# Expert results scattered to token order by GpSimd in the expert stage, and loaded by plain DMA later

## What is computed

```
x = layernorm(x + attn0(x))      # 16 heads of 64, a mask j < i + 64, behind a small MLP
x = layernorm(x + experts(x))    # 16 experts, each token goes to its best 4
x = layernorm(x + attn1(x))      # 16 heads of 8, low-rank additions to the weights
x = layernorm(x + recurrent(x))  # gated state, one step for each sequence

def experts(x):
    logits = -dist2(x, keys) + x @ rw.T + rb
    topv, topi = top_k(logits, 4);  w = softmax(topv)
    y_e = gelu(x @ w1[e].T + b1[e]) @ w2[e].T + b2[e]
    return sum_k w[k] * y_{topi[k]}
```

## Time and profile before

| | |
|---|---|
| median of 3 runs | 1423.19 us (1420.87 to 1427.43) |
| profiled execution, span from first to last instruction | 1445.1 us |
| its mean granted TensorE clock | 0.960 |
| busy: PE, DVE, ACT, POOL | 1272.4, 1014.5, 931.4, 770.7 us |
| DMA | 110.98 MB in 149016 packets |

### The profile page before, as it was taken

The page is one execution under the profiler, slowest core; times in us unless marked ns, Lnnn a source line. Parts: engine busy times, 40 slices in busy tenths (PEclk is TensorE's granted clock), DMA queues, the critical chain, the costliest instruction groups (busy, mean ns, idle before and its releaser), DMA issues.

```text
span 1445.1 us, 36685 instructions
## 1 busy us (share of the span) xinstructions
PE 1272.4 (88%) x9756; PEld 971.6 (67%) x9756; DVE 1014.5 (70%) x3763; ACT 931.4 (64%) x2825; POOL 770.7 (53%) x981
## 2 busy tenths in 40 slices
PE   7999999999999999984899998996787788788973
PEld 3777776777777777764899998993455455455652
DVE  2677777777777777775677776766787677678835
ACT  5878777777777778772465665653565555556644
POOL 1557777777777777775222121235466666664132
PEclk9999999999999999997899999997899989999997
DMA  9612222221112222221222223222323223222102
GB/s 340 206 60 74 73 73 73 73 73 54 47 51 72 69 71 71 73 74 58 62 71 82 77 82 90 81 79 65 80 58 78 67 53 85 58 61 64 36 1 59
DMA packets 149016, 110.98 MB, mean 77 GB/s; under 512 B 12833, under 2 KB 137249, under 8 KB 148770
## 3 DMA queue, kind: packets, MB, share of 16 engines
q1 hardware_dynamic: 139842, 92.45, 22.0%
q0 software_dynamic: 8192, 16.79, 4.1%
q10 hardware_dynamic: 864, 0.39, 0.1%
HBM read 47.27 MB, written 61.93 MB: 76 GB/s over the span
## 4 chain that ended last, share of the span: by engine, by line
PE 60%; DVE 10%; issue 8%; ACT 7%; another core or an unknown queue 4%; DMA 3%; SPq 3%; DVEq 3%; ACTq 1%; POOL 0%; POOLq 0%
PE psum L911 9%; PE psum L922 8%; PE psum L798 6%; PE psum L835 6%; PE psum L853 5%; PE psum L746 4%; PE psum L815 3%; PE psum L753 3%; PE psum L947 3%; PE psum L747 3%; ACT wall L1183 2%; PE psum L935 2%; PE psum L1018 2%; ACT P L1153 2%
## 5 line engine op out<-in xcount | busy, mean ns | idle before, releaser
L554 POOL TENSOR_SCALAR P<-P,rinv 128x192 f32<-128x192 f32 (+1 forms) x384 | 308.5, 816 | 158.7 <-DVE rinv L1335 151.7
L1153 ACT ACTIVATE P<-shifted,least 128x192 f32<-128x192 f32 (+1 forms) x512 | 240.2, 470 | 100.6 <-DVE least L1321 99.1
L1175 ACT ACTIVATE hid<-psum,wA 128x128 f32<-128x128 f32 x576 | 164.4, 368 | 123.8 <-PE psum L911 120.2
L1512 DVE TENSOR_REDUCE mx<-psum 128x2 f32<-128x512 f32 x256 | 165.2, 687 | 66.4 <-PE psum L1018 42.3
L1321 DVE CUSTOM_DVE_ANT_0 shifted<-psum,band 128x192 f32<-128x192 f32 (+1 forms) x512 | 168.9, 385 | 27.5 <-PE psum L798 27.2
L598 POOL DMA_INDIRECT yk<-xs,posc x128 | 125.6, 981 | 107.4 <-DVE wA L1473 57.6
L1183 ACT ACTIVATE wall<-psum 128x1024 f32<-128x1024 f32 x128 | 130.8, 1022 | 65.7 <-PE psum L935 47.5
L911 PE MATMUL psum<-xgT,wA 128*128 128x128 f32 x1152 | 156.0, 279 | 2.0 <-ACT hid L1175 1.4
L922 PE MATMUL psum<-wB,hid 128*128 128x128 f32 x1152 | 152.6, 276 | 0.0
L911 PEld LDWEIGHTS psum<-xgT,wA 128*128 128x128 f32 x1152 | 143.3, 195 | 3.2 <-ACT hid L1175 1.8
L835 PEld LDWEIGHTS psum<-ident,P 128*128 128x128 f32 x1024 | 117.6, 141 | 35.8 <-issue 29.4
(11 more groups left out here) (261 smaller groups left out, 2537.0 us busy)
## 6 DMA issues: line engine op xcount, KB each, us to landing
xs<-zrow SPq DMA_DIRECT2D x34, 1024.0 KB
xg<-xs SPq DMA_DIRECT2D x144, 64.0 KB, 1.8
xs<-yrow SPq DMA_DIRECT2D x144, 64.0 KB
wall<-in_wall SPq DMA_DIRECT2D x1, 8232.0 KB, 36.3
qkd<-parts SPq DMA_DIRECT2D x64, 96.0 KB
kst<-qkd SPq DMA_DIRECT2D x22, 128.0 KB
qst<-qkd SPq DMA_DIRECT2D x22, 128.0 KB
wall<-qkd SPq DMA_DIRECT2D x20, 128.0 KB
```

Of the source, the lines that this page charges most:

```text
L554: g.tensor_scalar(x, x, rinv[:, par, n:n + 1], None, ALU.mult).then_inc(s["pn_ready"], 1)
L1153: last = sc.activation(P[:, par, it, h, 0:w], shifted[:, par, it, h, 0:w], ACT.Exp, scale=-1.0, bias=least[:, par, n:n + 1], accum_out=row ...
L1175: sc.activation(hid[:, n % 4, f, :], up(n, f), ACT.Gelu, bias=wA[:, n % 4, F + f:F + f + 1]).then_inc(s["hid_ready"], 1)
L1512: v.tensor_reduce(out=mx[:, :, h], in_=SB[(par + 1 + h) % 3].rearrange("q (i n) -> q i n", i=TT), axis=mybir.AxisListType.X, op=ALU.max).t ...
```

## The change

Each row of `xs` gets a 129th word, the slot of its result: token times four plus k, behind 2048 spare slots. POOL writes these numbers once at the start (`slots`), copies two of them per partition into the rows before each pair of scatters, and waits for the earlier scatters before that copy and for the copy behind it. Unused rows are filled from `empty`, which is zero and has spare slot numbers. In the experts POOL scatters `yrow` by the slots that came with `xg` into a new DRAM tensor `yd` in token order, one indirect DMA a tile; SP no longer stores. `xg` has ten buffers, since the slots are read late. The gathers go: SP loads a batch of 256 tokens with its four results each from `yd` in one plain transfer (`fetch`), four batches in the expert stage and twelve at the start of steps of the second attention. POOL's other work of the expert stage is put between the scatters, tile by tile, and SP's first stack loads are dealt out in seven places. SP reads a tile's row number just before its load. DVE no longer copies `pos` to `pos_all`. The diff, cut to its core:

```diff
+RC = D + 1
+PITCH = RC
+SPILL = 2 * E * GT
+XG = 10
...
+        slots = sb("slots", [128, B, TT, TOPK], i32, c=a)
-        x1c = sb("x1c", [128, TT, D], c=a)
+        x1c = sb("x1c", [128, TT, RC], c=a)
+        empty = sb("empty", [128, E, RC], c=a)
-        xg = sb("xg", [128, 4, D], c=e2)
+        xg = sb("xg", [128, XG, RC], c=e2)
...
-        xs = nc.dram_tensor("xs", (ROWS, D), fp32, kind="Internal").ap()
+        xs = nc.dram_tensor("xs", (ROWS, PITCH), fp32, kind="Internal").ap()
+        yd = nc.dram_tensor("yd", (SPILL + TOK * TOPK, D), fp32, kind="Internal").ap()
...
-                sp.dma_start(rows[128 * c:128 * c + 128, :, :], nothing).then_inc(s["filled"], 16)
-            sp.dma_start(xs[DUMMY:ROWS, :].rearrange("(e r) d -> r e d", r=128), nothing[:, 0:NT - FULL, :]).then_inc(s["filled"], 16)
+                sp.dma_start(rows[128 * c:128 * c + 128, :, :], empty[:, :, :]).then_inc(s["filled"], 16)
+            spare_rows = xs[DUMMY:ROWS, :].rearrange("(e r) d -> r e d", r=128)
+            sp.dma_start(spare_rows[:, :, 0:D], zrow[:, :].rearrange("q (o d) -> q o d", o=1).to_broadcast([128, NT - FULL, D])).then_inc(s["filled"], 16)
+            sp.dma_start(spare_rows[:, :, D:RC], spare_slot[:, 0:NT - FULL].rearrange("q (e o) -> q e o", o=1).bitcast(fp32), allow_slow_non_contiguous=True).then_inc(s["filled"], 16)
...
             def load_rows(n):
                 need_alone(sp, "tin_mm", n - 3)
-                row[n] = row_of(n)
-                sp.dma_start(xg[:, n % 4, :], xs[bass.ds(row[n], GT), :]).then_inc(s[f"xg_in{n % 4}"], 16)
-
-            def store_rows(n):
-
-                need_alone(sp, "yrow_ready", n + 1)
-                need_alone(sp, f"ys_out{n % 2}", 16 * (n // 2))
-                sp.dma_start(xs[bass.ds(row[n], GT), :], yrow[:, n % 4, :]).then_inc(s[f"ys_out{n % 2}"], 16)
+                if n >= XG:
+                    need_alone(sp, f"ys_out{n % 2}", 16 * ((n - XG) // 2 + 1))
+                row = row_of(n)
+                sp.dma_start(xg[:, n % XG, :], xs[bass.ds(row, GT), 0:RC]).then_inc(s[f"xg_in{n % 4}"], 16)
+
+            def fetch(b, par):
+
+                need_alone(sp, "comb_done", b + 2)
+                sp.dma_start(yk[:, (par + 1) % 3, :, :], yd[bass.ds(SPILL + (b + 4) * N * TOPK, N * TOPK), :].rearrange("(q n) d -> q n d", n=TT * TOPK)).then_inc(s["yk_in"], 16)
+
+            def stored(n):
+
+                for k in range(2):
+                    sp.wait_ge(s[f"ys_out{k}"], 8 * n)
...
-                if n in (98, 100, 102):
+                if 98 <= n < 98 + 14 and n % 2 == 0:
                     load_stack(-2, 0, (n - 98) // 2)
+                for b, at in ((-4, 40), (-3, 72), (-2, 104), (-1, 136)):
+                    if n == at:
+                        stored(at - 8)
+                        fetch(b, b % 3)
+            stored(NT)
 
             def attention(b, par):
+                if has(b, 4) and not (isinstance(b, int) and b < 0):
+                    fetch(b, par)
...
-                        for k in (2 * p, 2 * p + 1):
+                        need_alone(pool, "scat", 16 * TT * (TOPK * (b - 2) + p))
+                        g.tensor_copy(rows_of(b - 2)[:, :, D:RC].bitcast(i32), slots[:, bass.ds(b - 2, 1), :, p:p + 1].rearrange("q o i k -> q (o i) k")).then_inc(s["slot_ready"], 1)
+                        need_alone(pool, "slot_ready", TOPK * (b - 2) + (p + 1))
+                        for it in range(TT):
+                            n = TOPK * it + p
                             nc.gpsimd.indirect_dma_start(
-                                out=xs, out_offset=bass.IndirectOffsetOnAxis(pos[:, k:k + 1], 0),
-                                in_=rows_of(b - 2)[:, k // TOPK, :], in_offset=None).then_inc(s["scat"], 16)
+                                out=xs, out_offset=bass.IndirectOffsetOnAxis(pos[:, n:n + 1], 0),
+                                in_=rows_of(b - 2)[:, it, :], in_offset=None).then_inc(s["scat"], 16)
...
             def outputs(b, par):
                 deviations(b)
-                fetch(b, par, 0)
+                gates_of(b, par)
                 keep(b)
                 combine(b, par)
                 new_state(b)
-                fetch(b, par, 1)
...
+            def scatter(n):
+
+                need_alone(pool, "yrow_ready", n + 1)
+                need_alone(pool, f"ys_out{n % 2}", 16 * (n // 2))
+                g.indirect_dma_start(out=yd, out_offset=bass.IndirectOffsetOnAxis(xg[:, n % XG, D:RC].bitcast(u32), 0),
+                                     in_=yrow[:, n % 4, :], in_offset=None).then_inc(s[f"ys_out{n % 2}"], 16)
...
+            for n in range(NT):
+                scatter(n)
+                clear_ahead(n)
+                for b, first in ((-5, 37), (-4, 69), (-3, 101), (-2, 133)):
+                    if n == first:
+                        gates_of(b, b % 3)
...
-                        v.tensor_copy(pos_all[:, bass.ds((b - 1) * TT * TOPK, TT * TOPK)], posf[:, :])
```

More of the change, by code:

```diff
@@ L568, in ones_rows, with gates_of @@
                 g.memset(kst[k][MROW:MROW + NPART, h:h + count, :], 1.0)
[L570 to L605 removed]
+            def gates_of(b, par):
+                if has(b, 5):
+                    need_alone(pool, "comb_done", b + 3)
+                    g.tensor_copy(gcur[:, (par + 2) % 3, :], gate_all[:, bass.ds(b + 5, 1), :].rearrange("q o k -> q (o k)")).then_inc(s["gates_in"], 1)
             def deviations(b):
@@ new lines, in combine_ahead, with clear_ahead @@
+                if piece == TT:
+                    g.tensor_tensor(acc, y4[:, :, 0, :], y4[:, :, 1, :], ALU.add)
+                if piece == TT + 1:
+                    g.tensor_tensor(acc, acc, x_all[:, (b + 4) * TT:(b + 5) * TT, :], ALU.add).then_inc(s["comb_done"], 1)
+            def clear_ahead(piece):
+                if piece < 16:
+                    x, h = (qst, kst)[piece // 4 % 2][piece // 8], 4 * (piece % 4)
+                    g.memset(x[:, h:h + 4, :].rearrange("q h n -> q (h n)").bitcast(fp32), 0.0)
+                elif piece < 24:
+                    if piece == 16:
+                        g.drain()
+                    ones_rows((piece - 16) // 4, 4 * (piece % 4), 4)
+                elif piece < 30:
+                    if piece == 24:
+                        g.drain()
+                    g.memset(v32[:, (piece - 24) // TT, piece % TT, :, :], 0.0)
+                elif piece == 30:
+                    g.drain()
+                    g.memset(v32[:, :, :, :, DH1:DH1 + 1], 1.0).then_inc(s["cleared"], 1)
@@ new lines, in scatter @@
+            def scatter(n):
[3 more added lines that the diff above has]
+                                     in_=yrow[:, n % 4, :], in_offset=None).then_inc(s[f"ys_out{n % 2}"], 16)
+            pool.sem_inc(s["x3_kept"], 1)
+            for n in range(NT):
+                scatter(n)
[3 more added lines that the diff above has]
+                        gates_of(b, b % 3)
+                for b, first in ((-4, 63), (-3, 95), (-2, 127)):
+                    if first <= n < first + TT + 2:
+                        combine_ahead(b, n - first)
+                for b, first in ((-3, 73), (-2, 107)):
+                    if n == first:
+                        deviations(b)
+                    if n == first + 7:
+                        keep(b)
@@ L1225, in weigh @@
                 slot, count = (par + 1) % 3, TT * TOPK // 2
-                need(act, f"yk_in{half}", 16 * count * (b + 5))
+                need(act, "yk_in", 16 * (b + 5))
                 need(act, "gates_in", b + 5)
```

165 lines of the change are left out of this document (46 added, 119 removed).

## The result

The changed kernel takes 1596.69 us (median of 4 runs, 1593.58 to 1604.3) against 1425.31 us for the kernel before on the same chip: ratio 1.1207, 95% interval 1.1173 to 1.1241. The sign is as forecast; 1597 us lies far above the range of 1430 to 1512 us.

The account below looks back on a forecast made before the run. PE was taken to bound the first attention, with POOL setting the pace nowhere. First attention 43 + between stages 11 - experts 6 - second attention 2 = +46 us of span, +45 on the median: 1468 us, range 1430 to 1512.

Parts of the forecast that it names:

- The sign: Whole kernel: the change makes it slower, +45 us on the median; slower had a chance of 0.86.
- The copy chain: First attention: slot copies before scatter pairs cost POOL 0.85 us more per step, stalling PE 1.75 us a batch.
- The wait for landing: First attention: scatters landing within the fill make step 3 another 1.7 us later, costing PE 1.4 us with weight loads.
- the fill drags: Rival, first attention: the fill costs 5 us a batch and more, 1495 to 1510 us in all; chance 0.13.
- Between the stages: First attention to experts: the last two batches' scatters show every landing and copy, +11 us (7 to 15).
- The experts: Expert stage: PE's three waits for rows go, -6 us; POOL's scatters cost nothing (0 to +15).
- the rival drawn from the Trainium skill: Experts: scatters' descriptors wait for VectorE's copies, 2.26 us a tile against 1.93, +47 on top, 1514 us; chance 0.07.
- The second attention: Second attention: POOL loses 96 gathers, SP gains 12 loads; -2 us (0 to -9, and +5 if loads delay maxima transfers).

Follow-up runs that it names:

- the best version: Changed kernel with later fill, rows kept four times, clearing every second tile, loads in four, load behind stacks, drains replaced by semaphores: 1411.97 us, ratio 0.9904 to before.
- The run that was to single out POOL's time: Kernel before without the second attention's gathers, a 776-word memset on POOL in place of each: 1424.53 us, ratio 0.9967.
- the second profile of before: The kernel before profiled once more, unchanged: 1429.33 us, span 1427.5 us, second attention 451.2 us.

## Why the prediction was wrong

**The copy chain: right.** 1.75 us a batch was worked out from POOL's order, 24.5 us for 14 batches. With the fill out of the way the loss was 25.2 us, and the wait of 0.82 us behind the copies is as forecast.

**The wait for landing: the step that failed.** "Shifted by 2.12 us it starts at 317.34, still within the fill, and lands near 322.4": this took over the 4.5 to 5.3 us that a scatter needed in the fill of before, and priced the wait at 1.7 us, the loss at some 1.35 us a batch, 19 us in all. It was 123.5 us. Three things were off. First, a scatter that starts later within a pair of fills of full speed does not keep its delay: 7.7 us in the run with rows 768 bytes apart, a wait of 4.33 us instead of 1.7. Its packets went out between 309.8 and 311.2 us, and POOL went on at 312.37; the forecast had the landing end with the packets. Second, the fill of 516-byte rows was not the fill of before: nearly 13 us instead of some 8, a scatter 11.7 us under way, a wait of 8.3 us: 55.0 us of the total. Third, the sum has no term for the clock in the first attention. Behind each long wait PE's granted clock stood at 0.50 for 7 to 10 us, and a batch's work took 41.13 us of PE instead of 38.87 with the later fill. This is in the 68.5 us that the first error cost: 40.0 of them are PE's waits, and by PE's busy time some 30 are the clock (an estimate, 2.2 us a batch in 14 batches).

**The rival "the fill drags"** had the mechanism, with a chance of 0.13, and a price that was half the true one: it let each fill last half as long again, which is near what it did, but priced that at 5 us a batch. POOL and PE had nothing to give back, so the whole lengthening of the landing came on top of the first error. The Trainium skill (DMA: Bandwidth & Descriptors, section How a descriptor splits into AXI transactions) says that the first transaction of a descriptor that does not start at a multiple of 256 bytes starts at the multiple below, and that the bytes before the start still cost. By its way of counting (an estimate) a row of 516 bytes takes three transactions at either pitch, since it starts at a multiple of 4 bytes, with 17 to 24 beats of 32 bytes at a pitch of 516 and 17 at 768. The two GB/s lines bear the direction out: the fill lands after 13.9 and 9.7 us. That the unaligned fill runs at 290 GB/s for its first 1.7 us does not follow from that count, and what makes it fall then was not settled.

**Between the stages: right**, +14.2 us for a forecast of +11 (7 to 15). With rows kept four times it was gone.

**The experts: wrong in sign.** The forecast saw that memsets and sums make single tiles too long, and let four row buffers take that up; its upper bound, +15 with POOL falling behind while it clears, is near what came. It did not see the drains. Behind a scatter they cost 1.4 to 3.5 us of POOL, 18.6 us in all, and with them 11.2 us of the stage. The gain that the forecast saw in the waits for rows was small even without them: 284.6 us against 285.7 in the best version. That scatters would starve beside VectorE's copies, the rival drawn from the Trainium skill (SBUF — State Buffer, section SBUF: two separate sides), is not what happened: 142 scatters of that stage averaged 984 ns, as the gathers had the earlier trace rows, and in the best version the stage with all its scatters is no longer than before.

**The second attention: the reason failed.** "No wait of PE names POOL" was read as if the gathers cost next to nothing, -2 us for the whole stage. Taking them out is worth 24 us of time, 27.6 of that stage. How they cost it is open: with them POOL has hardly any rest, PE waits for its stacks for 21.9 us in 1050:1320 us instead of 10.8, and its granted clock there is 0.97 instead of 1.00. The run that was to single out POOL's time slowed VectorE instead. The plain loads, beside which POOL rests for 8 to 12 us in most steps, took 13.7 us back (423.6 to 437.3), which leaves the 13.9 us. By the other pairs of profiles the gain is as small as 3.5 us, so that it lies above the forecast's 0 to 9 is not shown.

**The sum.** Forecast 43 + 11 - 6 - 2 = +46 us. Against the second profile of before the first expert rows came 163.3 us later (853.9 and 690.6), the experts took 14.8 more, the second attention 13.9 less: +164.2 us, the difference of the spans. Of the 118 us that the forecast missed, 104 are the landing (123.5 less 19), the clock behind it included.

## What to carry to other kernels

Before a wait for an indirect DMA's landing is put on an engine's list, look at what else the DMA queues do at that moment: a bulk transfer in the same 10 us sets the wait, and moving that transfer costs one number. A wait that stops PE costs more than its own length where the clock falls behind it. When a word is added to a row in DRAM, price the bulk transfers of those rows at the new pitch, not only by their bytes. And a stand-in that gives back the time of what it replaces need not have the same cause: before believing it, compare each engine's rests and the durations of its instructions.

## What the runs showed of the hardware

- Rows of 516 bytes at a pitch of 516 bytes were written at 290 GB/s for 1.7 us and then much slower, so that 2 MB took nearly 13 us; at a pitch of 768 bytes they kept near 290 to the end.
- A scatter of 128 rows that was issued as a 2 MB pair of fills began was waited for until 7.7 us after its start at a pitch of 768 bytes and 11.7 us at 516.
- Around a wait of PE of 7.2 us the granted clock stood at 0.50 (1.2 GHz) for 10.2 us, and eight transposes took 1.97 us instead of 1.04.
- A cast on VectorE (128 x 512, fp32 to bf16) that began beside four memsets on GpSimd took 2.78 us instead of 0.43 and ended 0.27 us behind them.
- A drain on GpSimd behind an indirect DMA left it idle for 1.4 to 3.5 us; with a semaphore from the operation that it guards the list of waits shows none there.
- Two profiles of the same kernel differed by 15 us in one stage, half of what was to be explained there.
